# ScalarE's visits in a state-space and feed-forward kernel: one gelu moved, X filled earlier, the second norm scaled by ScalarE instead of VectorE

## The reference, cut to what matters

```python
# 32 sequences of 256 tokens, 128 channels; D_INNER = 256, D_STATE = 16
xz = x @ W_in.T;  x_ssm, z = split(xz, 2)
x_ssm = silu(causal_conv4(x_ssm) + conv_b)
proj  = x_ssm @ W_x.T                     # B (16), C (16), one column for dt
dt    = softplus(proj[..., -1:] * W_dt[:, 0] + b_dt)
# per token: h = exp(dt*A) * h + (x*dt) * B;   y = sum over states of h * C
y = (y + x_ssm * D_param) * silu(z)
x = layernorm(x + y @ W_out.T)            # first norm
h = silu(tlin(x, w1)) * tlin(x, w2)       # 128 -> 512
h = gelu(tlin(h, h1));  h = gelu(tlin(h, h2))   # 512 -> 512, twice
x = layernorm(x + tlin(h, w3))            # 512 -> 128, second norm
```

## Time and profile before

| | |
|---|---|
| median of 3 runs | 1022.49 us (1021.69 to 1024.41) |
| the profiled execution | 1023.24 us, its span 1021.5 us |
| PE busy in the span | 964.2 us (94%) |
| DVE | 933.3 us (91%) |
| ACT | 895.5 us (88%) |
| POOL | 877.9 us (86%) |
| table loads on ACT | 44 at L618, 43 at L515, 15 at L769, 14 at L753, 1283 ns each |
| TensorE clock | 1.0 from slice 5 of 40 on |

### The profile page before, as it was taken

How to read it: one execution, slowest core, us unless ns; L and a number is a source line. 1 busy time by engine, 2 the same in 40 slices (tenths; PEclk the granted TensorE clock), 3 DMA queues, 4 the chain that set the end, 5 groups by cost and what they waited for, 6 DMA issues and landing times.

```text
span 1021.5 us, 13699 instructions
## 1 busy us (share of the span) xinstructions
PE 964.2 (94%) x3874; PEld 427.3 (42%) x3874; DVE 933.3 (91%) x1117; ACT 895.5 (88%) x1496; POOL 877.9 (86%) x529
## 2 busy tenths in 40 slices
PE   7947899999999999999999999999999999999998
PEld 3213344353444435353443435344443535334454
DVE  4799999999999999999999999999999999999500
ACT  5397899999999999999999999999999999997342
POOL 3489998989999898999999898999989899988420
PEclk8687999999999999999999999999999999999999
DMA  7959394884939496693949679493949769393000
GB/s 223 249 172 276 108 290 119 221 226 130 275 100 280 111 265 177 172 268 95 273 105 268 157 207 239 120 273 103 291 109 241 203 152 267 97 275 90 0 12 11
DMA packets 110717, 185.18 MB, mean 181 GB/s; under 512 B 12976, under 2 KB 23728, under 8 KB 110640
## 3 DMA queue, kind: packets, MB, share of 16 engines
q1 hardware_dynamic: 110112, 183.98, 67.9%
q10 hardware_dynamic: 528, 0.32, 0.1%
HBM read 162.23 MB, written 22.02 MB: 180 GB/s over the span
## 4 chain that ended last, share of the span: by engine, by line
issue 35%; DVE 33%; ACT 15%; PE 10%; POOL 6%; DMA 0%; DVEq 0%; POOLq 0%; ACTq 0%; SPq 0%
DVE hb L861 18%; DVE U L850 13%; ACT dA L515 6%; PE GY L947 5%; POOL pb L407 3%; ACT L515 2%; ACT L618 2%; ACT hid L618 1%; ACT X L524 1%; PE GY L938 1%; DVE conv L790 1%; DVE x L806 1%; PE GY L1003 1%; ACT GY L611 1%; POOL xds L397 1%
## 5 line engine op out<-in xcount | busy, mean ns | idle before, releaser
L407 POOL TENSOR_TENSOR pb<-hb,crep 128x1024 f32<-128x1024 f32 x256 | 602.1, 2362 | 50.9 <-DVE hb L861 46.5
L861 DVE TENSOR_TENSOR_SCAN hb<-dA,U 128x512 f32<-128x512 f32 x512 | 594.7, 1204 | 0.0
L515 ACT ACTIVATE dA<-dtr,negA 128x510 f32<-128x510 f32 x500 | 323.2, 714 | 8.2 <-DVE hb L861 7.0
L850 DVE TENSOR_TENSOR U<-X,xdr 128x512 f32<-128x512 f32 x500 | 320.0, 688 | 6.9 <-ACT X L524 5.0
L947 PE MATMUL GY<-g,h_sb 128*128 128x512 f32 x512 | 234.2, 601 | 0.0
L947 PE MATMUL GY<-hid,h_sb 128*128 128x512 f32 x512 | 228.3, 599 | 0.9 <-ACT g L760 0.7
L947 PEld LDWEIGHTS GY<-g,h_sb 128*128 128x128 f32 x512 | 93.5, 190 | 138.2 <-issue 138.2
L947 PEld LDWEIGHTS GY<-hid,h_sb 128*128 128x128 f32 x512 | 93.9, 190 | 135.7 <-issue 125.4
L938 PE MATMUL GY<-pb,sel_sb 128*32 128x512 f32 x1024 | 140.2, 620 | 8.0 <-POOL pb L407 7.9
L469 POOL TENSOR_TENSOR hid<-hid,g 128x512 f32<-128x512 f32 x64 | 80.8, 1276 | 8.9 <-ACT g L760 8.4
L951 PE MATMUL GY<-x1T,w_sb 128*128 128x512 f32 x128 | 68.6, 618 | 0.0
(11 more groups left out here) (136 smaller groups left out, 1061.0 us busy)
## 6 DMA issues: line engine op xcount, KB each, us to landing
dtr<-scr_dt SPq DMA_DIRECT2D x252, 256.0 KB, 8.1
xdr<-scr_xd SPq DMA_DIRECT2D x252, 256.0 KB, 7.7
brep<-scr_rows SPq DMA_DIRECT2D x32, 256.0 KB, 7.0
crep<-scr_rows SPq DMA_DIRECT2D x32, 256.0 KB, 8.8
scr_dt<-dts SPq DMA_DIRECT2D x32, 256.0 KB, 4.8
scr_xd<-xds SPq DMA_DIRECT2D x32, 256.0 KB, 4.9
xres<-xT_d SPq DMA_DIRECT2D x16, 256.0 KB, 9.8
xT_sb<-xT_d SPq DMA_DIRECT2D x15, 256.0 KB, 4.3
```

What stands on the lines that cost most here:

```text
L407: nc.gpsimd.tensor_tensor(pb[:, qs:qs + 2, :], hb[:, hs:hs + 2, :], crep[:, b % 2, g:g + 1, :].to_broadcast([P, 2, TB]), ALU.mult).then_in ...
L515: nc.scalar.activation(halves(dA[:, decay_slot(b, u), :])[:, :, 1:SEQ], halves(BREP[q] if by_product(b, k) else dtr[:, slot, q, :])[:, :, ...
L850: nc.vector.tensor_tensor(U[i][:], X[:], xdr[:, slot, q + i, :], ALU.mult).then_inc(s_u, 1)
L861: nc.vector.tensor_tensor_scan(hb[:, 2 * (v % H_PAIRS) + i, :], dA[:, decay_slot(j, u), :], U[i][:], 0.0, ALU.mult, ALU.add).then_inc(s_h, 1)
```

## The change

Six moves, all in rounds with a front, and one piece of work that changes engine:

1. The second norm's product by row goes from VectorE (one [128x512] product, L806) to ScalarE (`scale_rows`: four [128x128] copies with a scale per partition), in step 7 (step 9 where there is no front). The product of the block in round 16 stays on VectorE.
2. The gelu visit of step 4 goes. Row 2 of h2 joins the visit of step 1 as an instruction of its own, and row 3 is done in step 6, ahead of the silu of the gates. TensorE's `down` is split to match: rows 0 to 2 in step 4, row 3 after the first up projection.
3. fill 0 of X stands ahead of the two first taps (it stood after them and one decay), fill 1 ahead of the two decays of step 3.
4. The silu of the convolution stands behind the first gate and up pair.
5. Exp of the softplus waits for Abs alone, and one decay stands between Exp and Ln.
6. TensorE's third sum group of a round stands after the up projections; VectorE's tap goes from step 0 to step 1.

```diff
-        BH2_2 = (GY[:, 1:3, :], GY[:, 0:2, :])
+        BH2_2 = GY[:, 1:3, :]
...
-            def softplus_logs(b, c):
-                act.wait_ge(s_pre, 4 * b - 4 + 2 * c + 2)
+            def softplus_logs(b, c, meanwhile=None):
+                act.wait_ge(s_pre, 4 * b - 4 + 2 * c + 1)
                 nc.scalar.activation(soft[:, c, :], soft[:, c, :], ACT.Exp, scale=-1.0).then_inc(s_soft, 1)
+                if meanwhile is not None:
+                    meanwhile()
...
+            def scale_rows(b):
+                act.wait_ge(s_rs2, 2 * b + 2)
+                for t in range(NT):
+                    last = nc.scalar.activation(yo[:, t, :], tile_of(BW3, t), ACT.Copy, scale=rs2[:, t:t + 1])
+                last.then_inc(s_yo, 1)
...
                     if v == 9 and scan and not front:
+                        scale_rows(T)
                         fill_X(j, 2)
...
                         conv_first(I)
+                        if back:
+                            fill_X(A, 0)
                         tap_first(I)
...
                         copy_rows(A)
+                        if tail:
+                            scale_rows(T)
                         softplus_lines(A, 0)
-                        softplus_logs(A, 0)
+                        softplus_logs(A, 0, lambda: decay(j, 2 * v + AHEAD))
+                    if v == 3 and scan and j > 0:
+                        fill_X(j, 1)
...
-                            gelu(g2, flat(BH2_2[0]), s_h2, s_g2, T, 0, 2)
+                            gelu(g2, flat(BH2_2), s_h2, s_g2, T, 0, 2)
+                            gelu(g2, BH2[2], s_h2, s_g2, T, 2, 1)
...
-                    if v == 4 and tail:
-                        if scan:
-                            gelu(g2, flat(BH2_2[1]), s_h2, s_g2, T, 2, 2)
-                        else:
-                            for m in (2, 3):
-                                gelu(g2, BH2[m], s_h2, s_g2, T, m, 1)
+                    if v == 4 and tail and not front:
+                        for m in ((3,) if scan else (2, 3)):
+                            gelu(g2, BH2[m], s_h2, s_g2, T, m, 1)
...
+                        if tail and front:
+                            gelu(g2, BH2[3], s_h2, s_g2, T, 3, 1)
                         for m in range(NH) if back else ():
+                            if m == 1 and front:
+                                act.wait_ge(s_tap, taps_before(A + 1))
+                                act.wait_ge(*((s_tap1, 3 * A - 6) if tail else (s_conv1, A + 1)))
+                                nc.scalar.activation(flat(xs[:, A % 2, :, :]), flat(conv[:]), ACT.Silu).then_inc(s_xs, 2)
...
-                        if v == 9 and tail:
-                            scaled(yo, BW3, rs2, s_rs2, 2 * T + 2).then_inc(s_yo, 1)
...
-                    if v == (0 if tail else 1) and front and j > 0:
+                    if v == 1 and front and j > 0:
                         taps(A)
...
-                pe.wait_ge(s_g2, 4 * b + 4)
-                for k in range(NH):
+                for k in ks:
+                    pe.wait_ge(s_g2, 4 * b + k + 1)
...
-                    if v >= (3 if j > 0 else 7) and v % 2 and scan:
+                    if v >= (3 if j > 0 else 7) and v % 2 and scan and not (v == 7 and back):
                         sum_group(j, (v - 3) // 2)
...
-                        down(T)
+                        down(T, range(NH - 1 if front else NH))
...
                         up_proj(F, 0)
+                        if tail and front:
+                            down(T, range(NH - 1, NH))
...
+                    if v == 7 and back and scan:
+                        sum_group(j, (v - 3) // 2)
```

More of the change, by code:

```diff
@@ L680, in run @@
                         copy_rows(A)
+                        if tail:
+                            scale_rows(T)
                         softplus_lines(A, 0)
-                        softplus_logs(A, 0)
+                        softplus_logs(A, 0, lambda: decay(j, 2 * v + AHEAD))
+                    if v == 3 and scan and j > 0:
+                        fill_X(j, 1)
                     for u in (2 * v + AHEAD, 2 * v + AHEAD + 1):
-                        if u < TILES and scan:
+                        if u < TILES and scan and not (front and (v, u) in ((7, 2 * 7 + AHEAD), (9, 2 * 9 + AHEAD))):
                             decay(j, u)
@@ L690, in run @@
                             gelu(g1, flat(BH1_2[1]), s_h1, s_g1, F, 2, 2)
-                        if u == 34 and front:
+                        if u == 34 and front and not (intake and back):
                             fill_X(A, 0)
@@ L695, in run @@
                             gelu(g1, BH1[m], s_h1, s_g1, F, m, 1)
-                    if v == 3 and scan and j > 0:
-                        fill_X(j, 1)
                     if v == 3 and back:
@@ L771, in run @@
                         softplus_lines(A, 1, lambda: fill_X(j, 2))
-                        softplus_logs(A, 1)
+                        softplus_logs(A, 1, lambda: decay(j, 2 * (v + 1) + AHEAD))
                     if v == 15 and intake and not back:
@@ L972, in add_x1, with down @@
                                      skip_group_check=True)
-            def down(b):
+            def down(b, ks):
                 pe.wait_ge(s_w3c, 1)
-                pe.wait_ge(s_g2, 4 * b + 4)
-                for k in range(NH):
+                for k in ks:
+                    pe.wait_ge(s_g2, 4 * b + k + 1)
                     for t in range(NT):
@@ L980, in down @@
                                                 start=False, stop=(k == NH - 1), skip_group_check=True)
-                last.then_inc(s_w3, 1)
+                if NH - 1 in ks:
+                    last.then_inc(s_w3, 1)
             def out_proj(b):
```

4 lines of the change are left out of this document (removed).

## The result

The changed kernel takes 1016.51 us (median of 5 runs, 1016.1 to 1017.39) against 1023.24 (5 runs, 1021.69 to 1025.77) for the kernel before: a ratio of 0.9933, 95% interval 0.9916 to 0.9951. It is faster, by 6.7 us, more than the 0.3% that a measurement tells from no change. The profiled execution took 1016.1 us, its span is 1014.2; of before it was 1023.24 and 1021.5, so the two traces differ by 7.3 us of span.

The account below looks back on a forecast made before the run. VectorE is nearly full, but a loop through ScalarE, VectorE and TensorE sets the 58.50 us period. 12 x 0.74 = 8.9 plus 0.6 took 1023.24 to 1013.7, less 0.75 to the median: 1013.0 us, range 1004 to 1021.

Parts of the forecast that it names:

- 12 full periods: Rounds 2 to 13 carry the full change; each period falls from 58.50 to 57.76 us, 8.9 us together.
- round 14 to 15: This period ran at VectorE's own rate and loses the second norm's product: 0.6 us less.
- From the gelu to the norm's product: First part of the loop: fill wait gone, square sums later, first norm's product able to start 24.13 us after the gelu.
- The fill of step 4: ScalarE's fill of X for step 4 comes 0.7 us earlier and does not decide.
- From the product to the next gelu: Second part of the loop, through ScalarE's decays, gelu, silus, copies and softplus and TensorE: 33.63 us.
- The ring: Ring of 10 tiles stops ScalarE in step 6: second decay waits for a scan, until 4.15 us after the norm's product.
- the dearer switch: Rival: a ScalarE table switch costs more than its row's 1.32 us; period 59.1, time 1029 us, chance 0.02.
- the loop: Path gelu, square sums, power, norm's product, ScalarE's visits, TensorE, next gelu; sets the period at 57.76 us, forecast chance 0.50.
- VectorE's rate: Rival: VectorE without waits sets the period, 57.10 us, if the loop is 0.7 shorter; time 1005.1 us, chance 0.27.
- The copies at nothing: Copies' waits cost nothing: power ready over 3 us before, TensorE's softplus wait covers delay; without cover at most 1.07 us.
- The waits at the gates: Rival: ScalarE still waits for TensorE at the gate projections, 1.34 us not saved; period 59.1, time 1029.1 us, chance 0.09.
- No change: Rival: half the gate waits stay or the copies stall for a late power; period 58.3 to 58.6, 1019.5 to 1023 us, chance 0.12.

Follow-up runs that it names:

- kernel 5: The first norm's square sums moved ahead of the two decays of step 3, against the kernel of Experiment 1: 1009.06 us, and 1008.85 us in a second run.
- experiment 4: The four copies of rounds 2 to 14 made twice, the first set unused, against the kernel of Experiment 1: 1023.71 us, ratio 1.0006.
- Experiment 1: The second norm's product of round 15 put back on VectorE, rounds 2 to 14 unchanged, against the changed kernel: 1012.69 us, ratio 0.9898.
- experiments 3: Only the second norm's product of rounds 2 to 14 moved to ScalarE copies, nothing reordered, against the kernel before: 1032.74 us, ratio 1.0096.
- kernel 2: The second norm's product on VectorE in every round, so the reordering alone, against the kernel of Experiment 1: 1016.99 us, ratio 0.9938.
- kernel 6: Fill 0 of X put back behind the two taps and a decay, against the kernel of Experiment 1: 1015.95 us, ratio 0.9930.
- kernel 9: Fill 1 of X moved ahead of the two decays of step 2, against kernel 5: 1009.97 us, ratio 0.9883.
- kernel 8: TensorE's residual and rows 0 to 2 of the third layer ahead of the turn in round 15, against the kernel of Experiment 1: 1012.14 us, ratio 0.9903.
- kernel 7: Row 3's gelu back in a visit of its own in step 4, one table load more a round, against the kernel of Experiment 1: 1014.26 us, ratio 0.9917.

## Why the prediction was right, point by point

The time, 1016.5, lies 3.5 above the forecast of 1013.0 and inside the range; the sign and the mechanism of the full rounds were right. Of the 3.5, 0.75 is the step from the profiled execution to the median, which fell away (over five runs the median of the kernel before is 1023.24, that of its profile), 0.4 the same step after (1016.1 to 1016.5), and 2.4 are the saving itself. Two errors of opposite sign hide in it, and that they cancel by half is luck. By the prediction's steps, with the saving of the span:

| term | forecast | measured |
|---|---|---|
| 12 full periods | 12 x 0.74 = 8.9 | 12 x 0.95 = 11.4 |
| round 14 to 15 | 0.6 | 57.06 - 56.49 = 0.6 |
| start, rounds 1 and 2 | 0 | 0.66 (scatter) + 0.18 = 0.8 |
| round 15 to 16 | 0 | -5.6 |
| end | 0 | 0.1 |
| sum | 9.5 | 7.3 |

*From the gelu to the norm's product.* Forecast G + 24.13, measured 505.08 - 480.98 = 24.10. The fill's wait went and the power became what VectorE waits for, 0.12, less than the 0.2 to 0.4 that I named. The square sums started at G + 21.58, as forecast. The fill of step 4, said not to decide, was late for VectorE as well, by 0.17 (U at 501.43, where 499.02 + 2.24 = 501.26 had been free of waiting); behind it the product would have waited for the power all the same, so it did not set the period. In kernel 5, where the power comes earlier, it does.

*From the product to the next gelu.* Forecast 33.63, measured 538.53 - 505.08 = 33.45. The ring stopped the second decay at x + 4.22 (4.15 forecast), the first silu came at x + 8.16 (8.05), the waits at the gate and up pairs went whole, the copies cost 1.00 (1.07). Two switches of the new visit are in the rows: gelu from the end of a decay in 1.31 (510.02 to 511.33), silu from the end of the gelu in 1.31 (511.93 to 513.24). That is the load of 1.28 and 0.03 of handover. The Trainium skill (ScalarE: Activation LUTs, What ACT_TABLE_LOAD costs) adds a drain of 1380 ns to each switch; neither of these two shows it, and the dearer switch as a rival is out.

*The period.* 57.76 was forecast and 57.55 measured (24.10 + 33.45). The two halves were over by 0.03 and 0.18; of the 0.18, 0.07 are the copies, and the rest is not traced to a term. Twelve times 0.21 is the 2.5 by which the loop term is too small. That the loop sets the period and VectorE's rate does not, which was the prediction's main choice between 57.8 and 57.1, is shown by experiment 4: 1.00 us of copies more, 1.00 us of period more. That VectorE's rate lies just behind is shown by experiment 5, where 57.33 is, to 0.02, the 57.13 of that rate (56.49 of round 14 to 15, plus 0.64 for the tap) and the 0.18 for fill 1.

*The copies at nothing.* In the round shown this held: the copies follow the row copy at 521.47 with no wait for the power, and of TensorE's hidden blocks only the third waits, for softplus, 0.59 where it was 0.54. But the cover ahead of TensorE's first block was the 0.42 above, and not the 3 us that the power was early.

**The step that failed**, in a forecast that held as a whole, is this sentence: "The rest (the first two rounds, the feed-forward tail after the scan) I cost at nothing: the tail is TensorE's chain and gets no shorter." It got longer, by 5.6 us, before the tail had begun. The cover for the copies (the power ready over 3 us before ScalarE comes to them, and TensorE's blocks later still) I had read from a full round. In round 15 TensorE has no projections ahead of its first hidden block and reached it 17.10 behind the product before, in a full round 18.56. And the diff has the copies there in another step, behind a table load, four decays and the start of the sums: they start 19.96 behind the product (926.83 - 906.87), in a full round 16.57 (521.65 - 505.08). So in place of 0.42 to spare there were 2.98 to wait, and the price that the prediction gives for the case without cover, "at most the 1.07 of the copies", was too low as well. Experiment 1 shows that this one line costs 4.6 us of the 5.6: 2.98 of wait and the lower clock behind it. The remaining 1.0 goes with the lower clock at the turn: it is there in every profile with that fall, and in none without (last section). Had I costed the line, from ScalarE's list, at the 3.0 of the wait, the forecast would have been 1016.0; the 1.5 of the clock, and the 1.0 of the turn, no row shown of before could have told.

*The rivals.* VectorE's own rate: excluded for this kernel by experiment 4, though kernel 5 comes near it. The waits at the gates: gone. No change: the period went well below 58.3. The dearer switch: out, as above. The copies do cost what they take wherever the list has no air (experiments 3 and 4), but the reordering had made room for the first four.

## What to carry to other kernels

Read the period of a pipelined kernel from one instruction in two rounds, and walk the loop through the engines; moving work to the less busy engine pays only as far as the loop through it has air at that place before the move. The same four copies gained 4 us in one order and cost 10 in the other, and four more of them cost 11 in the first. Cost a moved piece in every kind of round, the incomplete ones at the end above all: the cover that hides it in a full round may not exist there, and one round gave back 5.6 us of 12.8. A fill of a single buffer has a window, too late it stalls its reader, too early it stalls everything that is queued behind it (experiments 2, 6, 9).

## What the runs showed of the hardware

TensorE's granted clock fell from 1.00 to 0.50 at waits of 2.67 (turn of round 15) and 2.92 us (first hidden block) in the changed kernel, and a block of 24 matmuls took 12.11 in place of 10.57. At the turn of round 15 eleven profiles can be compared (kernel 8 has other work there):

| | wait at the turn, us | product to third sum group, us |
|---|---|---|
| the clock falls: changed kernel, kernels 1, 2, 6, 7, 9 | 2.67, 2.66, 3.22, 2.66, 2.47, 2.82 | 17.13 to 17.34 |
| it stays at 1.00: kernel before, kernels 3, 4 and 5 (two profiles) | 2.84, 1.86, 1.87, 2.67, 2.66 | 16.09 to 16.11 |

In kernel 9 the clock was 1.00 for the first 1.2 us after the wait (905.80 to 907.00) and then 0.54 and 0.61 to 911.00. In kernel 5 it was 1.00 behind the wait too:

```profile
904.30:906.00 1.70, 1.63 (x15) 1.63 (x16) 1.70 (x4) 1.69 (x2) 1.70 (x1) 1.00 1.07 261
```

So a wait of 2.5 to 3.7 us can cost 1.0 to 1.7 us more than itself (the 1.70 is that of experiment 8, after 3.68), and whether it does isn't told by its length alone. What decides stays open. It may differ between executions of one kernel, which these profiles, one for each run, don't show. Two executions of kernel 2 with a mean granted clock of 0.980 took 1014.84 us each, the four with 0.975 to 0.976 took 1016.52 to 1018.13. Both profiles of kernel 5 are executions with 0.980 and the shortest of their runs (1007.33 and 1006.94); the six others, with 0.976 to 0.978, took 1008.41 to 1009.86. So the 1 us that kernel 5's profile gains in round 15 is not to be counted to its square sums.

The four copies with a scale per partition took 1.00 us from start to start of what is behind them (0.25 each), where the only one in the trace before took 0.367 with nothing behind it.
